# Routing work of the first mixture stage moved into the second feed-forward stage, and seven gathers into the routing phase

## What is computed

```python
x = x + 0.5 * lora_ffn(norm(x))      # base 128x128 + gated sum of 8 rank-8 products
x = x + attention(norm(x))           # 16 heads of 8, relative bias, causal softmax
x = x + 0.5 * lora_ffn(norm(x))      # same weights: "second feed-forward stage"
x = x + 0.5 * moe(norm(x))           # first mixture stage
x = x + retention(norm(x))           # 8 heads
x = x + 0.5 * moe(norm(x))           # second mixture stage

def moe(x):                          # 16 experts in 4 groups
    s = sigmoid(x @ router) + bias
    keep the 2 groups whose two best s sum highest; of their 8 experts the 4 best by s
    w = 2.5 * score / sum of the 4 scores
    return sum over the 4 of w * (silu(x @ gate) * (x @ up)) @ down + shared expert(x)
```

## Time and profile before

| | us |
|---|---|
| median of 3 runs | 1351.33 |
| the profiled execution | 1355.15 |
| its span, first to last instruction | 1353.4 |
| PE busy | 1261.7 (93%) |
| DVE busy | 964.7 (71%) |
| ACT busy | 765.2 (57%) |
| POOL busy | 765.6 (57%) |

### The profile page before, as it was taken

One profiled execution on the slowest core, in us unless ns is written; L12 is line 12 of the kernel. 1 busy time (PEld: TensorE's weight loads), 2 busy tenths in 40 slices (PEclk: granted clock), 3 DMA queues, 4 the chain that ended last, 5 costly groups with the idle time before them and its releaser, 6 DMA issues. The chain is left out here.

```text
span 1353.4 us, 34803 instructions
## 1 busy us (share of the span) xinstructions
PE 1261.7 (93%) x10236; PEld 1074.6 (79%) x10236; DVE 964.7 (71%) x4100; ACT 765.2 (57%) x1805; POOL 765.6 (57%) x1010
## 2 busy tenths in 40 slices
PE   7899999998867799999779999999999979999998
PEld 5667777776746688888669999998988867888887
DVE  6678888887759455656458787888888847555554
ACT  2288888885364244444246667776677654444443
POOL 2288888885333645555335556575687554345543
PEclk9899999998878899999979999999999989999999
DMA  5199980000030112121112212121221112112121
GB/s 149 36 274 272 270 258 0 0 2 2 1 117 32 58 29 30 30 29 28 22 46 54 52 50 51 44 55 44 57 60 49 31 38 81 35 28 32 30 30 15
DMA packets 102887, 85.27 MB, mean 63 GB/s; under 512 B 10791, under 2 KB 90505, under 8 KB 102490
## 3 DMA queue, kind: packets, MB, share of 16 engines
q1 hardware_dynamic: 84084, 65.51, 17.6%
q0 software_dynamic: 17280, 16.17, 6.8%
q10 hardware_dynamic: 1382, 1.83, 0.5%
HBM read 20.92 MB, written 45.78 MB: 49 GB/s over the span
## 5 line engine op out<-in xcount | busy, mean ns | idle before, releaser
L1973 POOL TENSOR_TENSOR attn_z<-attn_top,attn_z 128x256 f32<-128x256 f32 x256 | 154.1, 612 | 35.3 <-DVE attn_top L1923 34.6
L1923 DVE CUSTOM_DVE_ANT_0 attn_z<-banks,rel_bias 128x128 f32<-128x128 f32 (+1 forms) x512 | 147.3, 353 | 23.4 <-PE banks L2056 18.0
L2492 POOL TENSOR_TENSOR ret_rotated<-ret_twins 128x512 f32<-128x512 f32 x64 | 82.1, 1283 | 132.8 <-DVE ret_twins L2402 132.7
L997 DVE SCALAR_TENSOR_TENSOR moe_block_act<-banks,moe_block_weights,moe_block_gated 128x128 f32<-128x128 f32 x276 | 77.7, 344 | 65.5 <-ACT moe_block_gated L1052 40.3
L2006 ACT ACTIVATE attn_prob<-banks 128x384 f32<-128x384 f32 x256 | 111.7, 488 | 20.8 <-PE banks L2066 14.4
L1542 DVE SCALAR_TENSOR_TENSOR moe_block_act<-banks,moe_block_weights,moe_block_gated 128x128 f32<-128x128 f32 x276 | 77.7, 344 | 63.0 <-ACT moe_block_gated L1636 39.6
L2555 ACT ACTIVATE ret_normed<-banks,ret_head_shift,ret_head_rstd 128x128 f32<-128x128 f32 x256 | 96.3, 458 | 45.5 <-DVE ret_head_shift L2426 45.2
L2066 PE MATMUL banks<-ident,attn_z 128*128 128x128 f32 x768 | 111.2, 280 | 0.7
L2066 PEld LDWEIGHTS banks<-ident,attn_z 128*128 128x128 f32 x768 | 82.2, 140 | 20.8 <-issue 14.2
L2587 PE MATMUL banks<-ret_x_hi,ret_hi 128*128 128x256 f32 x256 | 85.1, 332 | 1.9 <-ACT ret_gate L2548 1.0
L1026 POOL DMA_INDIRECT y_rows<-moe_block_y,moe_taken x37 | 58.7, 1585 | 46.6 <-ACT moe_block_y L1062 38.5
(11 more groups left out here) (359 smaller groups left out, 4060.0 us busy)
## 6 DMA issues: line engine op xcount, KB each, us to landing
slots<-moe_pad SPq DMA_DIRECT2D x12, 2560.0 KB, 23.4
ret_twins<-ret_twins SPq DMA_DIRECT2D x256, 64.0 KB
moe_stage<-in_moe_w SPq DMA_DIRECT2D x4, 576.0 KB, 6.8
bias_reversed<-scratch SPq DMA_DIRECT2D x1, 2048.0 KB, 9.5
y_rows<-moe_pad SPq DMA_DIRECT2D x1, 2048.0 KB, 9.3
back_of_seq<-y_rows SPq DMA_DIRECT2D x16, 128.0 KB, 2.3
out<-x_res SPq DMA_DIRECT2D x8, 256.0 KB, 2.5
ret_stage<-in_ret_w SPq DMA_DIRECT2D x16, 96.0 KB, 2.1
```

The lines of the kernel that those rows point to most:

```text
L997: last = dve.scalar_tensor_tensor(act_f[:, i, at], ps_u[:, i, at], weights[:, s % 2, part, e:e + 1], gated[:, i, at], ALU.mult, ALU.mult)
L1923: last = dve.tensor_tensor_reduce(out=z[:, s, cols], in0=ps_s[:, i, cols], in1=bias, scale=1.0, scalar=-3.0e38, op0=ALU.add, op1=ALU.max, ...
L1973: pool.tensor_tensor(z[:, s, P:WIDTH], top[:, s, 1:2].to_broadcast([P, WIDTH - P]), z[:, s, P:WIDTH], ALU.subtract).then_inc(shifted1, 1)
L2492: pool.tensor_tensor(rotated[:, k % 2], twins[:, k % 2, 0], twins[:, k % 2, 1], ALU.add).then_inc(rotated_ready, 1)
```

## The change

- The routing front becomes a class of its own, `RouteHead`, whose stages are placed into the steps of the second feed-forward stage; the steps go on to 11 (`HEAD_STEPS`). In DVE's step the shift of group n-1 stands behind the feed-forward's layernorm, and the layer statistics of group n (new: a wait for that group's residual) and the split of group n-2 behind the residual. The router product has another form: 12 products of 16 columns for a group, straight into token-major logits, and no transposes back. One bank holds the transposes where there were two.
- The choice of the first half (`Choice`) goes in steps 7 to 10, 6 operations a step, its classes behind them.
- The four splits of expert weights move from steps 3 to 6 to steps -1 to 2 (`in_first_iteration`).
- The routing phase begins with the rank of the first half and its row numbers; the second choice goes beside tiles 0 to 7, places beside tiles 10 to 17. POOL issues the first seven gathers behind the wait for the scatters.
- SP issues the retention loads at the start of the blocks instead of the start of routing; each split of retention weights comes one place later (units 4 to 64, blocks 2 to 32).
- A barrier with `retire` that stood between front and routing now stands between routing and blocks. Tiles that are not alive together share one SBUF tensor (`Arena`).

Core of the diff:

```diff
+class RouteHead:
+        def vector(dve):
+            def shift_of(g, _):
...
+                dve.wait_ge(rstd_done, g + 1)
+                dve.scalar_tensor_tensor(shift[:, at], mv[:, at, 0], -1.0, rstd[:, at], ALU.mult, ALU.mult).then_inc(shift_done, 1)
+            def layernorm(g, _):
+                dve.wait_ge(after_ffn, g + 1)
+                dve.nop(nofuse=True)
...
+            return Steps(dve, GROUPS, 1, [(-1, shift_of), (0, layernorm), (-2, split_x)])
...
+            def set_tokens(g, _):
+                if g == 0:
+                    pool.wait_ge(after_attention, BATCHES)
...
+            return Steps(pool, GROUPS, 1, [(0, set_tokens), (0, inverse_std)])
...
+            return Steps(act, GROUPS, 1, [(-2, copy_x_hi), (-1, normalise), (-3, copy_logits)])
...
+            def router(g, _):
...
+                for j in range(GROUP):
+                    hi, lo = (part[:, g, j * P:(j + 1) * P] for part in (x_hi, x_lo))
+                    out = ps_logit[:, j * MOE_E:(j + 1) * MOE_E]
+                    pe.matmul(out, hi, r_hi, start=True, stop=False)
+                    pe.matmul(out, hi, r_lo, start=False, stop=False)
+                    last = pe.matmul(out, lo, r_hi, start=False, stop=True)
...
+            return Steps(pe, GROUPS, 1, [(-2, transpose_x), (-3, router)])
```

```diff
-            for n in range(GROUPS):
-                ffn2.at(n)
+            route = head.vector(dve)
+            for n in range(HEAD_STEPS):
+                ffn2.at(n, 0, 3)
+                route.at(n, 0, 1)
+                ffn2.at(n, 3)
+                route.at(n, 1)
+                if n == CHOICE_FIRST:
+                    choice.set_pads(dve)
+                if n >= CHOICE_FIRST:
+                    choice.topk(dve, 0, (n - CHOICE_FIRST) * 6, (n - CHOICE_FIRST) * 6 + 6)
+            choice.classes(dve, 0)
...
+            for n in range(-2, HEAD_STEPS):
+                ffn2.at(n, 0, 1)
+                route.at(n)
+                ffn2.at(n, 1)
...
+            for n in range(HEAD_STEPS):
+                ffn2.at(n, 0, 1)
+                route.at(n, 0, 1)
+                ffn2.at(n, 1, 3)
+                route.at(n, 1)
+                ffn2.at(n, 3)
...
+                if n == CHOICE_FIRST:
+                    act.wait_ge(head.logits_ready, SEG // GROUP)
+                    choice.sigmoid(act, 0)
                 ffn2.at(n)
+                route.at(n)
```

```diff
@@ moe_route: DVE, POOL, PE @@
+            row_numbers(0)
             done = 0
+            for i in range(0, choice.TOPK, 3):
+                choice.topk(dve, 1, i, i + 3)
+                shared(done, done + 1)
+                done += 1
+            choice.classes(dve, 1)
+            shared(done, done + 1)
+            row_numbers(1)
+            shared(done + 1, done + 2)
...
             pool.wait_ge(scattered, TILES * 16)
+            pool.wait_ge(places.placed, places.INDEX_AT)
+            for i in range(early.RB - 1):
+                early.gather(pool, i)
...
-            shared(0, 9)
             rank_tokens(0)
-            shared(9, 19)
+            shared(0, 11)
             rank_tokens(1)
-            shared(19, TILES)
+            shared(11, TILES)
@@ moe_blocks @@
         def _(sync):
+            background(sync)
...
-            for s in range(RB - 1):
-                gather(s)
...
-                if s % 2 == 0 and s // 2 < split[2]:
-                    split[1](pool, s // 2)
+                if s % 2 == 0 and 1 <= s // 2 <= split[2]:
+                    split[1](pool, s // 2 - 1)
...
-                if k % 4 == 0 and k // 4 < split[2]:
-                    split[0](act, k // 4)
+                if k % 4 == 0 and 1 <= k // 4 <= split[2]:
+                    split[0](act, k // 4 - 1)
@@ constants, placement of the expert splits @@
-LOOPS = 6
+LOOPS, HEAD_STEPS = 6, GROUPS + 3
+CHOICE_FIRST = SEG // GROUP + 3
...
-        if isinstance(it, int) and it == iterations - 1 and k < parts:
+        if isinstance(it, int) and it == 0 and k < parts:
```

More of the change, by code:

```diff
@@ L490, in moe_route @@
+def moe_route(nc, tag, banks, used, x_res, ident, w, slots, places, route, choice, early):
     I32 = mybir.dt.int32
@@ L809, in shared @@
                         copy_actT(t - 2)
-            normalise(0)
-            for g in range(GROUPS):
-                if g + 1 < GROUPS:
-                    normalise(g + 1)
-                copy_x_hi(g)
-                if g >= 1:
-                    copy_logitT(g - 1)
-            copy_logitT(GROUPS - 1)
-            sigmoid(0)
-            shared(0, 4)
-            sigmoid(1)
-            shared(4, TILES)
+            choice.sigmoid(act, 1)
+            shared(0, TILES)
             copy_actT(TILES - 2)
@@ L917, in _, with __init__, gather, moe_blocks @@
             down(TILES - 1)
-def moe_blocks(nc, tag, banks, used, ident, w, slots, y_rows, places, order, back_first, split):
+class Gathered:
+    RB = 8
+    def __init__(self, nc, ctx, tag, sems, slots, places, order):
+        self.taken = ctx.enter_context(nc.sbuf_tensor(f"{tag}_taken", [P, self.RB, ROW], F32, side="right"))
+        self.taken_ready = [new_sem(nc, sems, f"{tag}_taken_ready{i}") for i in range(self.RB)]
+        self.slots, self.places, self.order = slots, places, order
+    def gather(self, pool, s):
+        b, r = self.order.blocks[s], s % self.RB
+        rows = bass.IndirectOffsetOnAxis(self.places.index[:, b:b + 1], 0)
+        pool.indirect_dma_start(self.taken[:, r, :], None, self.slots, rows).then_inc(self.taken_ready[r], 16)
+def moe_blocks(nc, tag, banks, used, ident, w, y_rows, places, early, background, back_first, split):
     I32 = mybir.dt.int32
-    RB, RX, RY = 8, 3, 3
+    order, taken, taken_ready, gather = early.order, early.taken, early.taken_ready, early.gather
+    RB, RX, RY = early.RB, 3, 3
     ORDER, UNIT_OF, FIRST_UNIT, LAST_UNIT = order.blocks, order.unit_of, order.first, order.last
@@ L944, in moe_blocks @@
         ps_x, ps_y = bank([P, 512])[:, 0:P], bank([P, 512])[:, 0:C]
-        taken_ready = [sem(f"taken_ready{i}") for i in range(RB)]
         y_scattered = [sem(f"y_scattered{i}") for i in range(RY)]
@@ L1167, in __init__ @@
         self.kept_minus = sb("kept_minus", [P, N * MOE_G])
-        self.kept_score = sb("kept_score", [P, N, MOE_E])
+        self.kept_score = arena.take([P, N, MOE_E])
         self.masked = sb("masked", [P, N, MOE_E + MOE_K])
@@ L1172, in __init__ @@
         self.replaced = sb("replaced", [P, N, MOE_E + MOE_K])
-        self.picked = sb("picked", [P, N, MOE_E])
+        self.picked = arena.take([P, N, MOE_E])
         self.total = sb("total", [P, N])
@@ L2116, with front_phase @@
 LATE_FLIPS = {-5: (4, 5), -4: (6, 7)}
-LOOPS = 6
-def front_phase(nc, banks, used, x_res, first, attention, second, opening, background):
+LOOPS, HEAD_STEPS = 6, GROUPS + 3
+CHOICE_FIRST = SEG // GROUP + 3
+def front_phase(nc, first, attention, second, head, choice, opening, background):
     with ExitStack() as ctx:
```

481 lines of the change are left out of this document (237 added, 244 removed).

## The result

In 20 runs the changed kernel took 1348.99 us (median; 17 of them lie between 1343.3 and 1353.7, the other three, 2061 us and more, were disturbed and are in no ratio), the kernel before 1351.51 us in 20 runs. The ratio is 0.9973, 95% interval 0.9961 to 0.9985: 2 to 5 us faster. Forecast were 1339.5 us and a gain of 11.8. The profiled execution took 1349.05 us, its span is 1347.2 (before 1355.15 and 1353.4).

The account below looks back on a forecast made before the run. PE was taken to bound the blocks, so an earlier start ends the kernel earlier: 400.7 + 57.2 = 457.9 for the first block transpose instead of 469.73, 11.8 us less, median 1339.5 us; range 1332 to 1350.

Parts of the forecast that it names:

- Part 3: PE beside DVE in the merged stage: half clock in steps 2 and 3, full from step 4; DVE waits 2.4 us.
- T: Start of the routing phase, the first rank product, ending the merged stage; forecast at 400.7 us against 402.3 before.
- Part 1: DVE's work in the merged feed-forward stage: 55.2 us from 335.17, so done at 390.4 if it never waited.
- Part 2: POOL's weight splits, moved to steps -1 to 2, hold up DVE there: 6.8 us in all, bounds 0 and 9.4.
- Part 4: Routing phase: PE ends at T + 55.1, last gather T + 55.3, block transposes T + 57.2; 10.2 us gained.
- Part 5: SP's loads moved from the routing front to the start of the blocks: cost 0, bounds -1 and +3.
- Rival A: Clock stays at half from step 2 to 6: T 415.6, transpose 3.1 us later than before, 1354.4; chance 0.16.
- half case: Merged stage, clock back at step 4's end: T 406 to 408, 1345 to 1347; chance 0.22 together with D.
- Rival B: Splits never hold DVE in the merged stage and PE keeps up: T 391.6 to 396, 1330.5 to 1335; chance 0.12.
- C: POOL's scatters start or land late, so POOL ends the routing phase: 1341.5 to 1343; no separate chance.
- D: Gathers behind the scatters only move the barrier wait: last 6.1 us stay, 1345; chance 0.22 together with the half case.

Follow-up runs that it names:

- r14: Changed kernel with each of POOL's four low-part weight splits issued as four subtractions, a repeat of r5; 1389.48 us, ratio 1.0008 to the kernel before.
- r13: r5 with all 32 POOL scatters of the routing phase issued only after the last add of shared work; 1409.4 us, ratio 1.0148 to the kernel before.
- r16: r14 with the seven gathers back at the start of the blocks; 1386.0 us, ratio 0.9985 to the kernel before.
- r10: Changed kernel plus 84 unread identity transposes on PE, ahead of steps 0 to 3 and in step 4; ratio 1.0042 to the kernel before.
- r2: Changed kernel with POOL's four low-part subtractions of expert weights replaced by a memset of zero; ratio 1.0006 to the kernel before.
- r5: Changed kernel with each of POOL's four low-part weight splits issued as four subtractions of 288 columns; ratio 1.0009 to the kernel before.
- r1: Changed kernel once more, no edit, on a chip other than the first; median 1395.7 us, ratio 1.0036 to the kernel before.
- r18: Kernel before with its 32 first-mixture-stage scatters issued after the last add of shared work; first to last shared product 60.7 us, no kernel time given.
- r4: Changed kernel plus 8 unread identity transposes on PE ahead of its first work in steps 1 to 3; ratio 1.0036 to the kernel before.
- r8: Changed kernel with only the seven gathers moved back to the start of the blocks; ratio 1.0027 to the kernel before.

## Why the prediction was wrong

It was wrong in one step, **Part 3**: "so I count steps 2 and 3 at it [...] and the full clock from step 4 on [...] the last product is done at about 382, DVE waits 2.4 us in all". PE took 11.1 us for step 3 (360.18 to 371.30), 7.1, 7.7 and 4.9 for steps 4 to 6; DVE waited 9.8, residual 7 began at 391.25. Of the 9.6 us by which T is late, 7.4 are these waits, 1.6 is DVE work ahead of residual 7 that was not counted (the waits taken off 391.25 leave 381.5, where my terms give 335.17 + 55.2 - 17.3 + 6.8 = 379.9; 0.3 of it is in the holds), 1.4 is a longer tail (18.7, not 17.3), and the barrier took 0.4, not 1.2. What the runs showed in place of the full clock from step 4 on: 0.50 for 37.6 of 47.8 us, up to 388.1. r14 against r13 and r16 shows what that costs, the same instructions with and without 13.5 us of it: 5.4 us of T. r10, with the same holds and the clock up, gets 5.1 back. With the full clock the forecast's waits were right (2.6 in r13, forecast 2.4), though r13's are for POOL's inverse root, a wait that the forecast does not name.

- **Part 1** (DVE's 55.2 us): 2.7 us short, the 1.6 and 1.4 just told less 0.3 of holds.
- **Part 2** (holds 6.8, from 2.1 + 1.3 + 1.3 + 2.1): 2.3 + 1.4 + 1.4 + 2.0 = 7.1. Right in size. Split 0 met the normalise, not the router shift. The trace of the kernel before had that row, and what follows from it, and the forecast passed over both: the normalise held beside the first split, and then PE waiting for it, with 0.50 from 360.9 on.

```profile
355.16 3.44 DVE L235 TENSOR_SCALAR ffn_xn<-x_res,ffn_mv,ffn_rstd 128x128 f32<-128x128 f32 x4
358.66 0.66 PE L291 MATMUL banks<-ident,ffn_xn 128*128 128x128 f32 x4 [2.28 <-DVE ffn_xn L235]
```

So I took the holds for a cost of DVE's time alone, where they also let PE run dry. With fewer holds T falls by more than the holds are shorter: 9.2 for 5.5 us of holds in r2, 9.6 for 3.7 in r5 (starts equal). That they fed the low clock fits this and is not shown: with the pieces the clock fell at 350.5 to 353 as well, in every trace, and only what came behind differed. The Trainium skill's rule (SBUF — State Buffer, Who interferes with whom: an exclusive lock, the later one waits) would by my working have had about 5 us of holds, where 7.1 were measured; that DVE gets in between short pieces agrees with it.

- **Part 4**: T + 55.7 for PE's end (forecast 55.1), last gather's end T + 54.7 (55.3), block transpose T + 58.0 (57.2). Right within 0.8 us, on the chip of the first measurement. With stalls it fails by 35 us.
- **Part 5** (loads at the start of the blocks cost nothing): PE had no wait for a gather or a y scatter there. Right.
- **Rival A** came in most of its length: last product 391 where A had 397, T 410.4, under its 412.5, so "below that the change gains" held. Its half case said 1345 to 1347 with 22% beside D. I set its chance too low because a PE that is the bound is always busy. The trace shows a PE at 0.50 and busy for 21.7 of the 22.4 us from 352 to 374.4, and for all of 377.8 to 388.1; being busy did not bring the clock back at once. The rule of the Trainium skill (TensorE: Matmul & The Clock Gate, Part 1) that sustained activity releases the throttle made A look unlikely; these 22 us speak against leaning on it.
- **Rival B** (T 391.6 to 396) did not come even where the holds are cut (r13: 399.05, with 3.4 us of holds left). **C** and **D** did not come: POOL ended 0.9 us before PE; the block transposes waited for no gather.

With T late by 9.6 the forecast's own sum gives 1349.1; the median is 1348.99. That they agree so closely is luck: the block transpose came 1.4 us earlier than before, and the median fell by 2.5, with stretches of the clock behind the transpose that no term of the sum has.

## What to carry to other kernels

A POOL instruction that holds DVE up is best issued in short pieces: four of 0.76 us held DVE for 0.6 to 1.1 us where one of 2.6 held it 1.4 to 2.3. Count every instruction that the pieces meet, not only the first. When one engine is held up, ask what its idle neighbour's clock does next, and do the sum with the low clock to the end of the stage as well as with the high one. Take more than one trace before a difference of a few us in a landmark is laid to an edit: here the same instructions gave landmarks 5.4 us apart. Work put beside a train of POOL's indirect DMAs may be safe on one chip and stall on the next; a gain of 1% that rests on it should be measured on several.

## What the runs showed of the hardware that I had not expected

- On all five further chips, indirect DMAs from POOL (128 rows each, every 1.68 us on average in r1) went with stalls of up to 9 us in instruction issue on PE, DVE and ACT, 35 us in a routing phase of the changed kernel, and none with the DMAs moved behind the other work (r13 and r18, on two of these chips).
- With transposes of the identity that nobody reads in its idle stretches, PE stayed at 1.00 until 360 in place of 347 (r4), and had 0.99 from 373 to 389 (r10).
- The clock's stretches in one order of work can repeat from chip to chip (T 410.36, 410.72, 410.29) and yet are not fixed by it: r8, with the same instructions up to T, came to 408.4 with starts equal, and the same pieces gave 398.8 (r13, r16), 400.8 (r5) and 404.2 (r14).
